# A fused convolution and adapted linear layer in FP32, on one core: one Strassen step over sample pairs and halves of both matrix dimensions

## What is computed

```
conv = conv1d(x, weight, 9 taps, 4 groups of 32 channels) + c @ c_weight.T + bias   # (32,128,2048)
h    = conv.reshape(8, 512, 2048)                                  # 8 batches of 4 samples
A_eff[b], B_eff[b] = mixes of lora_A, lora_B by gate[b]            # rank 32, plus one shared pair of rank 32
ffn  = h @ kernel + ffn_bias + (h @ A_eff.T) @ B_eff.T + (h @ A_shared.T) @ B_shared.T
out  = x + ffn                                                     # kernel is 2048 x 2048
```

## Time and profile before

| what | us |
|---|---|
| median of 3 runs | 1988.12 |
| lowest and highest | 1986.23, 1988.28 |
| span of the profiled execution | 1986.6 |
| TensorE busy in it | 1928.7 (97%) |
| VectorE, ScalarE, GpSimd busy | 800.3, 601.5, 175.6 |
| moved between HBM and SBUF | 177.11 MB, 89 GB/s |

### The profile page before, as it was taken

The page is one execution under the profiler, slowest core; times in us unless marked ns, Lnnn a source line. Parts: engine busy times, 40 slices in busy tenths (PEclk is TensorE's granted clock), DMA queues, the critical chain, the costliest instruction groups (busy, mean ns, idle before and its releaser), DMA issues.

```text
span 1986.6 us, 24464 instructions
## 1 busy us (share of the span) xinstructions
PE 1928.7 (97%) x9996; PEld 1646.8 (83%) x9996; DVE 800.3 (40%) x1115; ACT 601.5 (30%) x928; POOL 175.6 (9%) x70
## 2 busy tenths in 40 slices
...
DMA packets 100687, 177.11 MB, mean 89 GB/s; under 512 B 56752, under 2 KB 69840, under 8 KB 87504
## 3 DMA queue, kind: packets, MB, share of 16 engines
...
## 4 chain that ended last, share of the span: by engine, by line
PE 92%; DMA 4%; DVE 2%; ACT 1%; issue 0%; SPq 0%; ACTq 0%; DVEq 0%
PE acc L802 67%; PE cps L696 14%; PE acc L819 3%; PE cps L792 3%; PE cps L706 3%; DMA w_raw<-in_L_ffn_kernel 2%; PE acc L746 1%; PE cps L773 1%; DMA w_raw<-mixed_B 1%; ACT cv_xq L399 1%; DMA stage<-in_L_ffn_lora_A 0%; DVE w_lo L506 0%; ACT w_hi L382 0%; PE cps L768 0%; DVE cv_xq L516 0%
## 5 line engine op out<-in xcount | busy, mean ns | idle before, releaser
L802 PE MATMUL acc<-w_hi,y_t 128*128 128x512 f32 x4096 | 1037.0, 391 | 5.5 <-DVE w_lo L506 5.5
L802 PEld LDWEIGHTS acc<-w_hi,y_t 128*128 128x128 f32 x4096 | 763.8, 188 | 174.0 <-issue 13.0
L802 PE MATMUL acc<-w_lo,y_t 128*128 128x512 f32 x2048 | 549.6, 390 | 0.0
L802 PEld LDWEIGHTS acc<-w_lo,y_t 128*128 128x128 f32 x2048 | 385.6, 188 | 81.8
L399 ACT COPY cv_xq<-x_raw 32x257 f32<-32x257 f32 x512 | 329.2, 643 | 9.5 <-DMA x_raw<-in_x 2.7
L412 ACT CAST y_t<-cps 128x1024 fp32r<-128x1024 f32 x64 | 65.0, 1016 | 851.3 <-PE cps L706 850.8
L360 POOL TENSOR_TENSOR stage<-stage,bias_half 128x1024 f32<-128x1024 f32 x32 | 94.6, 2957 | 1789.2 <-DMA stage<-out 1789.2
L696 PE MATMUL cps<-x_hi,cw_hi 128*128 128x256 f32 x768 | 224.7, 293 | 11.7 <-DVE x_lo L523 11.7
L673 DVE TENSOR_TENSOR stage<-acc,stage 128x2048 f32<-128x2048 f32 x32 | 73.3, 2292 | 366.6 <-PE acc L819 366.6
L696 PE MATMUL cps<-x_hi,cw_lo 128*128 128x256 f32 x768 | 219.0, 285 | 0.0
L696 PE MATMUL cps<-x_lo,cw_hi 128*128 128x256 f32 x768 | 218.7, 285 | 0.0
...
## 6 DMA issues: line engine op xcount, KB each, us to landing
out<-stage SPq DMA_DIRECT2D x64, 1024.0 KB, 4.4
...
stage<-out SPq DMA_DIRECT2D x32, 1024.0 KB, 6.5
w_raw<-in_L_ffn_kernel ACTq DMA_DIRECT2D x64, 256.0 KB, 2.7
...
w_raw<-in_L_ffn_lora_B SPq DMA_DIRECT2D x16, 256.0 KB, 7.0
w_raw<-mixed_B SPq DMA_DIRECT2D x16, 256.0 KB, 8.6
mixed_A<-x_raw SPq DMA_DIRECT2D x2, 1024.0 KB, 5.4
```

Of the source, the lines that this page charges most:

```text
L802: ins = T.matmul(acc[:, m, :], y_t[:, ch, part, :], wt[:, ch, m * 512:(m + 1) * 512], start=(ch == 0 and part == 0 and wt is w_hi), stop=( ...
```

## The change

The samples are taken in 16 pairs, l and the columns in two halves each. So there is a product of 2 x 2 blocks, A (samples of a pair by halves of l) times B (halves of l by halves of columns). One Strassen step in Winograd's form computes it with seven block products and not eight. The kernel runs them as phases 0 to 6, each over all 16 pairs: 112 units `u = 16 f + p`. A unit is one sample-sized left block by one combined quarter of W, that is 8 chunks x 3 part pairs x 2 column blocks = 48 matmuls (L1073). `acc` now holds two buffers of two banks, used in turn.

- Right factors `T_OF`: phases 0, 1 and 6 use a quarter of W as it is; phases 2, 3, 4 and 5 use sums of 4, 3, 2 and 2 quarters. SP loads the quarters' chunks (L334, L340), GpSimd adds them (L545: 56 adds of 128x1024), ACT and VectorE split the sum into the chunk slots. There are 12 slots for 8 chunks, so chunks 0 to 3 of the next phase are split in units 2, 4, 6 and 8 of this one and chunks 4 to 7 after its last unit.
- Left factors: phases 0 to 2 use A11, A12 and A22 straight from the convolution; these are also stored to HBM (L464). The convolution of A21 is made for phase 3 and only enters sums: S1 = A21 + A22 and S2 = S1 - A11 on VectorE (L804, L811), S3 = A11 - A21 and S4 = A12 - S2 with their signs on GpSimd (L573, L575). Phase 3 multiplies S2 and stores S1, S3 and S4, which phases 5, 4 and 6 load again (L428).
- The turned convolution is first copied by ACT from PSUM to SBUF (`y_raw`, L630), and the high part (L645) and low part (L796) are taken from SBUF.
- Results: intermediate sums E1, E4, U2, U3 and U4 go to HBM and come back. Phases 1, 4, 5 and 6 finish a quarter of the output; there GpSimd adds the bias and x (L553, L556). In phases 4 and 5 the low-rank part goes to a PSUM buffer of its own, and VectorE makes three adds (L956, L959, L963 or L965).
- The A-side product is made in phases 0, 1, 2 and 4, the B-side one in 1, 4, 5 and 6. Both keep their number of matmuls: 64 x 8 and 256. The convolution and the turn keep theirs too, and are made in phases 0 to 3.
- lora_B is mixed in phase 0, a piece in each unit. All loops are written out; before, most steps were in hardware loops.

The core of the diff, TensorE's part:

```diff
-                for ch in range(NCH):
-                    for part, wt in ((0, w_hi), (0, w_lo), (1, w_hi)):
-                        for m in range(MB):
-                            ins = T.matmul(acc[:, m, :], y_t[:, ch, part, :], wt[:, ch, m * 512:(m + 1) * 512],
+            for u in range(NU):
+                f, p, b = u // NP, u % NP, u % 2
...
+                if u >= 2:
+                    pe.wait_ge(evac_done, u - 1)
+                for c in range(NCH):
+                    k = NCH * f + c
+                    if p == 0:
+                        pe.wait_ge(w_lo_ready, k + 1)
+                    for part, wt in ((0, w_hi), (0, w_lo), (1, w_hi)):
+                        for m in range(2):
+                            ins = T.matmul(acc[:, b, m, :], y_buf[b][:, c, part, :],
+                                           wt[:, k % SLOTS, m * 512:(m + 1) * 512],
...
+                    if c == 3 and u + 1 < NCV:
...
+                        turn(u + 1)
...
+                if u + 2 < NCV:
+                    conv(u + 2, unit)
```

The right factors, and the sums of phase 3 on VectorE, SP and GpSimd:

```diff
+T_OF = [[(B11, 1)], [(B21, 1)], [(B21, 1), (B22, -1), (B12, 1), (B11, -1)], [(B22, 1), (B12, -1), (B11, 1)],
+        [(B22, 1), (B12, -1)], [(B12, 1), (B11, -1)], [(B22, 1)]]
...
+                V.tensor_tensor(g[:, 1], g[:, 1], g[:, 0], ALU.add).then_inc(s1_ready, 1)
+                dve.wait_ge(s1_ready, vp + 1)
+                dve.wait_ge(s_blk_in[1], 16 * (vp + 1))
...
+                V.tensor_tensor(s2_buf[:], g[:, 1], g[:, 4], ALU.subtract).then_inc(s2_ready, 1)
...
+                    for i, (d, b) in enumerate(((A22_d, 1), (A11_d, 4), (A12_d, 5))):
+                        if vp >= 1:
+                            sp.wait_ge(s_out[i], 16 * vp)
+                        sp.dma_start(g[:, b], d[vp]).then_inc(s_blk_in[i], 16)
...
+                    V.tensor_tensor(g[:, 4], g[:, 4], g[:, 0], ALU.subtract).then_inc(s3_ready, 1)
+                    pool.wait_ge(s_blk_in[2], 16 * (vp + 1))
+                    V.tensor_tensor(g[:, 5], g[:, 5], s2_buf[:], ALU.subtract).then_inc(s4_ready, 1)
```

More of the change, by code:

```diff
@@ L195, in build @@
         ax_lo_ready = sem("ax_lo_ready")
-        ax_stored = sem("ax_stored")
+        ax_out = sem("ax_out")
         axp_in = sem("axp_in")
+        axs_in = [sem(f"axs_in{i}") for i in range(2)]
         bs_in = sem("bs_in")
@@ new lines, in load_b, with load_shared_b @@
+            def load_b(u):
+                f, b = u // NP, u % NP // 2
+                cols = slice(0, HALF) if f in (1, 4) else slice(HALF, L)
+                for rows in (0, R2):
+                    sp.dma_start(b_raw[rows:rows + RANK, :], mixed_B.rearrange("(b r) k m -> b (r k) m", b=NB)[b][:, cols]
+                                 ).then_inc(b_in, 16)
+            def load_shared_b(half):
+                cols = slice(half * HALF, (half + 1) * HALF)
+                for rows in (RANK, R2 + RANK):
+                    sp.dma_start(b_raw[rows:rows + RANK, :], shared_B[:, cols]).then_inc(bs_in, 16)
@@ L356, in _ @@
-            pool.wait_ge(bias_in, 32)
-            with pool.Fori(0, NB) as i:
-                for j in range(SPB):
-                    pool.wait_ge(part_in, 16 * (4 * i + j + 1))
-                    nc.gpsimd.tensor_tensor(stage[:, 0:HALF], stage[:, 0:HALF], bias_half[:], ALU.add).then_inc(pre_added, 1)
-                    pool.wait_ge(x_in[j], 16 * (8 + i + 1))
-                    nc.gpsimd.tensor_tensor(stage[:, HALF:L], stage[:, HALF:L], x_raw[:, j, PAD:XW], ALU.add
-                                            ).then_inc(pre_added, 1)
+            V.affine_select(out=ident[:], in_=ident[:], compare_op=ALU.not_equal, fill=1.0, base=0,
+                            pattern=[[-1, P]], channel_multiplier=1).then_inc(id_ready, 1)
@@ new lines, in form_t @@
+            def form_t(f, j, part):
+                k = NCH * f + j
+                n = adds_before(f) + T_ADDS[f] * j + part
+                src, sign = (part - 1) % 2, T_OF[f][part][1]
+                before = sum(sum(1 for q in range(1, len(T_OF[e])) if (q - 1) % 2 == src) for e in range(1, f)) * NCH
+                each = sum(1 for q in range(1, len(T_OF[f])) if (q - 1) % 2 == src)
+                nth = before + each * j + (part - 1) // 2 + 1
+                if part == 1:
+                    pool.wait_ge(t_in[k % 4], 16 * (k // 4 + 1))
+                else:
+                    pool.wait_ge(t_formed, n - 1)
+                pool.wait_ge(tmp_in[src], 16 * nth)
+                V.tensor_tensor(st[:, k % 4], st[:, k % 4], st[:, 4 + src], ALU.add if sign > 0 else ALU.subtract
+                                ).then_inc(t_formed, 1)
@@ L495, in _ @@
-            phases(act, step)
+            x_split(0)
+            for j in range(4):
+                load_first_t(j)
+            for j in range(4):
+                split_t(0, j)
+            a_mixed_copy(0)
+            x_rearrange(1)
+            x_split(1)
+            act.wait_ge(as_copied, 1)
+            a_split(0)
+            y_raw(0)
+            y_hi(0)
+            for j in range(4, 6):
+                load_first_t(j)
+            a_mixed_copy(1)
+            for j in range(6, 8):
+                load_first_t(j)
```

1080 lines of the change are left out of this document (664 added, 416 removed).

## The result

The changed kernel takes 2047.8 us (median of 4 runs, 2043.1 to 2050.1) where the kernel before takes 1987.9 (4 runs, 1986.2 to 1988.3): a ratio of 1.0301, 95% interval 1.0286 to 1.0315. It is 60 us slower. The forecast was 1946, with a range that ended at 2035.

A forecast was written before the change was run, and what follows sets the result against it. TensorE was taken to bound the kernel (97% busy, 92% of the chain). Dense 1773 + 45 + 4 + 80 + 10 + 27 + 5 = 1944, so 1946 as median, since the profiled run stands 1.5 under it; range 1855 to 2035.

The forecast's parts named there:

- The dense part: Whole kernel without added waits: start 102, then phases 0 to 6 at 280, 287, 274, 247, 204, 189, 189; sum 1773.
- the lock: VectorE operations with two SBUF inputs and GpSimd adds exclude each other for whole instructions; 216 adds, 2.4 each.
- Phase 1's 45: Phase 1: w_lo, y_lo and x_lo take turns with GpSimd's adds, 38, plus first bias wait and clock; bounds 5 and 80.
- phase 2's 4: Phase 2: convolution due at 12.8, x_lo ends at 12 to 13; 4 in all.
- a chain of 24.3 or 18.6: Phase 3: compute ring through S2, S3, y_lo, S4, x_lo and convolution; 24.3 without an add for W, 18.6 with one.
- a transfers' ring of 20 to 23: Phase 3: evacuation, U2's store and landing, E1 and three S stores, wait, three loads; 20 to 23 a unit.
- 80 became 105: Phase 3: mean unit 21.5 instead of 16.06 gives 76, plus 4 for the last two units: 80; bounds 34 and 140.
- the 10 of the change: Change into phase 4: first S3 is loaded only after the last S4 is stored, y_lo 7 to 12 late; 10.
- Phases 4 and 5: 27: Waits of 1 a unit in phase 4 and 0.7 in phase 5, 16 + 11; bounds 0 and 110.
- A: Whole kernel: the waits hide, no lock meets the chain, transfers are early; 1825, chance 0.10.
- B: The lock rarely hits x_lo but the transfers' ring holds: phase 1 5, phase 3 68; 1893, chance 0.17.
- C: Slower: SP's queue carries phases 4 and 5, units 16.5 and 16, 99 more; 2045, decided from mean 14.6, chance 0.23.

The follow-up runs named there:

- the test: Changed kernel plus a test behind its last evacuation: seven kinds of VectorE operation alone, then beside three GpSimd adds; eight narrow copies 3.23, then 9.35 us.
- short adds: Changed kernel with every GpSimd add cut from 1024 to 16 columns, waits and transfers kept, part of the computation left out: 1939.2 us.
- S first: Changed kernel, full computation, with phase 3's S stores and block loads ahead of the wait for the evacuation in SP's queue: 2061.0 us.
- Early loads: Changed kernel, full computation, with a_raw's load at the top of the odd unit and the second bias half one unit earlier: 2011.3 us.
- the 1835 of the short adds: Kernel with x splits first, a_raw and bias early and S first, every GpSimd add cut to 16 columns, part of the computation left out: 1835.1 us.
- three moves: Changed kernel, full computation, with x splits ahead of y's, a_raw and bias loaded early, and phase 3's S stores and block loads first: 1910.1 us.
- W's add behind S: Kernel with three moves; in phase 3 x's load stands ahead of the S stores and GpSimd's W add behind S3 and S4: 1873.2 us.

## Why the prediction was wrong

**The dense part was right** (its terms add up to 1772 where the forecast has 1773, a rounding). Main matmuls went from 6144 to 5376 at the same pace, phase 0 took 282 (280 forecast), phase 6 190.0 (189), unit 1 started at 101.7 (102), the tail took 4.4 (5). Of the forecast's signs, "units 18.7 in phase 0" (18.8) and "phase 6 at 11.8" came true. Of the 102 that were missed, phases 1 and 2 have 40, phases 4 and 5 have 37, phase 3 with the change into phase 4 has 28.

**The step that failed: what the lock stops.** The forecast read from rows 7 that two SBUF inputs on VectorE and an add on GpSimd exclude each other, and priced w_lo, y_lo and x_lo by it. It took VectorE's eight copies of x (ACT does the other eight of a unit) to be free of the lock, since they have one input. The rows of the changed kernel (3.15 alone, 9.53 beside adds) and the test (3.23 and 9.35) show the contrary. A unit of phase 1 with all adds beside the copies loses 6 there, before any of the steps that were priced. With it W's adds cost 65 in all, 58 of it in phase 1, where the forecast had 38 there for all adds. No run frees the copies alone, so their share of this isn't measured. Phase 1's 45 became 71, inside the forecast's bounds of 5 to 80; phase 2's 4 became 18, of which some 12 are W's and other adds, as the runs with short adds show (279.1), and the first ring of S in its last unit, 24.7, is in it too.

**Phase 3: the mean of two rings.** The forecast had a chain of 24.3 or 18.6 and a transfers' ring of 20 to 23, and took 21.5 for a unit with a convolution. The ring of transfers was well sized: 21.3 with short adds. What failed is the mean: a unit can't be shorter than its longest ring, and these two share a piece. The evacuation, with which SP's queue begins, stands on VectorE behind y_lo and x_lo, so the lock's time lengthens both rings. Measured, the 14 units with a convolution take 23.3. Counted from unit start to unit start phase 3 has 111 beyond its dense 247, of which 6 are the wait at the change: 80 became 105, within 34 to 140, and the 10 of the change 6. The 18.6 of a unit with an add for W was not found in the changed kernel, whose units take 20.8 to 25.2; with S first, where W's add fell on S2, such a unit took up to 26.0.

**Phases 4 and 5: 27, without the change into phase 4, became 65** (457.7 against 393 without a wait). Early loads take 28 of that away in phase 4. The forecast counted bytes in these phases, 320 GB/s, and found them enough; they were, as far as the rows go (258 and 279 GB/s; with a_raw earlier, phase 4 did the same transfers in 221.2). What failed is its wait of 1 a unit: it did not ask where in SP's order the one small load stands that the next unit needs first. The diff had it.

**The rivals.** A is excluded. B (the lock rarely hits, 1893) is excluded by the 109 that short adds give back. C named 2045, and 2047.8 was measured, but not by its mechanism: it wanted phases 4 and 5 to take 99 more than the forecast's 421, a mean of 16.3 a unit, and called itself decided from 14.6; they took 37 more, a mean of 14.3. The number agrees by chance. What it says of SP's queue is right in kind, and the sign it named did appear: TensorE waits 3.41 for a y_lo behind a load in phase 4, and the evacuation 14.21 behind the bias in phase 5. The order in that queue costs 28 in phase 4, and phase 3's ring is closed by it. A rival for slower by the lock alone was missing. Its price could have been had from the forecast's own bounds: 80 in phase 1, 140 in phase 3 and all else as it stood give 2039. The range ended at 2035 and had no place for both at their upper ends; but phase 1's term and a good part of phase 3's had one cause, the lock, and went up together.

**What stays open.** Phase 5's first two units, 31 in place of some 24, wait for b_raw behind other loads; no run moved that load. And 1873 stands against the 1835 of the short adds (taken with three moves, not with W's add behind S): about that much GpSimd's adds still cost. No run tried to have fewer of them.
